# Four graph layers over 16 graphs on one core: degrees behind the wide drops, two row keys together, row numbers ahead of the next batch's scaling

## What is computed

```
layer 0: relu(D (A+I) D h W)          D = 1/sqrt(rowsum(A+I))
layer 1: [h, g h, g^2 h, g^3 h] W^T + b   g = d (A+I) d,  d = 1/(sqrt(rowsum)+1e-7)
layer 2: MLP(h + quantile aggregate of each node's neighbours)
         neighbours: A+I, from which rows with more than 10 neighbours lose every k-th one,
         in both directions; weighted sum of the 0.25, 0.5 and 0.75 quantiles, per feature
layer 3: A (h W) + b
```

## Time and profile before

| | us |
|---|---|
| median of 3 executions | 2806.65 |
| lowest, highest | 2795.49, 2807.34 |
| profiled execution, its own time | 2827.46 |
| its span, first to last instruction | 2825.7 |
| PE busy | 1535.0 (54%) |
| DVE busy | 1625.1 (58%) |
| ACT busy | 462.6 (16%) |
| POOL busy | 1299.3 (46%) |

### The profile page before, as it was taken

One profiled execution on the slowest core, in us unless ns is written; L12 is line 12 of the kernel. 1 busy time (PEld: TensorE's weight loads), 2 busy tenths in 40 slices (PEclk: granted clock), 3 DMA queues, 4 the chain that ended last, 5 costly groups with the idle time before them and its releaser, 6 DMA issues.

```text
span 2825.7 us, 24253 instructions
## 1 busy us (share of the span) xinstructions
PE 1535.0 (54%) x8885; PEld 858.3 (30%) x8997; DVE 1625.1 (58%) x2443; ACT 462.6 (16%) x756; POOL 1299.3 (46%) x1196
## 2 busy tenths in 40 slices
PE   3735637556374655638366464836636375565232
PEld 2412414323142332314233241423314243233111
DVE  2511827649285574928467383755828376494926
ACT  3101212102021120202112020210302121020000
POOL 1072370735527173552717447172643707265550
PEclk9766658667586766759577676866768586777555
DMA  3122130313213131321313123131322313112120
GB/s 99 54 25 53 46 55 21 75 11 86 19 40 62 24 75 12 83 22 34 67 20 77 15 53 54 29 69 8 88 18 50 55 22 75 10 23 20 23 24 4
DMA packets 106610, 120.13 MB, mean 43 GB/s; under 512 B 71486, under 2 KB 71614, under 8 KB 106430
## 3 DMA queue, kind: packets, MB, share of 16 engines
q0 software_dynamic: 36864, 37.82, 14.2%
q1 hardware_dynamic: 69566, 79.98, 9.2%
HBM read 109.27 MB, written 8.45 MB: 42 GB/s over the span
## 4 chain that ended last, share of the span: by engine, by line
DVE 40%; PE 24%; issue 18%; another core or an unknown queue 15%; ACT 2%; DVEq 1%; POOL 0%; DMA 0%; POOLq 0%; ACTq 0%; SPq 0%
PE ps_tr L596 7%; DVE lists L1181 4%; DVE slots L1001 4%; PE ps_tr L604 4%; DVE slots L1000 3%; PE ps_prod L615 3%; PE ps_tr L585 2%; PE ps_misc L775 2%; DVE slots L1008 2%; DVE slots L1009 2%; DVE xc L977 1%; DVE stat L979 1%; DVE stat L976 1%; PE ps_misc L704 1%
## 5 line engine op out<-in xcount | busy, mean ns | idle before, releaser
L403 POOL DMA_INDIRECT slots<-h_rows,row_no x1152 | 1287.4, 1118 | 1433.2 <-DVEq L1187 1087.0
L596 PE MATMUL ps_tr<-adj_t,y_mid 128*128 128x512 bf16 x960 | 301.7, 459 | 223.7 <-issue 121.3
L1223 DVE TENSOR_TENSOR y_mid<-ps_prod,scales 128x512 f32<-128x512 f32 x48 | 33.2, 692 | 554.2 <-remote 407.5
L448 ACT ACTIVATE columns_t<-ps_tr 128x512 f32<-128x512 f32 (+1 forms) x192 | 113.0, 595 | 1409.2 <-PE ps_tr L604 888.7
L596 PEld LDWEIGHTS ps_tr<-adj_t,y_mid 128*128 128x128 bf16 x1024 | 105.6, 112 | 471.1 <-issue 416.0
L1181 DVE MAX8 lists<-ps_key 128x8 f16<-128x1024 f32 x128 | 157.8, 1233 | 112.8 <-PE ps_key L685 69.4
L585 PE MATMUL ps_tr<-h_t,w_l_sb 65*128 65x512 f32 x192 | 151.3, 896 | 107.6 <-issue 76.1
L695 PE MATMUL ps_misc<-parts_w,select_t 128*128 128x64 bf16 x384 | 36.7, 220 | 268.1 <-issue 229.3
L472 ACT ACTIVATE adj_n<-adj_f 128x1024 f16<-128x1024 f32 x128 | 134.3, 1050 | 229.1 <-remote 80.7
L604 PE MATMUL ps_tr<-adj_t,low 128*64 128x512 bf16 x1024 | 157.9, 419 | 16.9 <-issue 16.6
L615 PE MATMUL ps_prod<-both_ident,columns_t 128*128 128x64 f32 x768 | 107.9, 297 | 101.6 <-issue 91.6
(11 more groups left out here) (210 smaller groups left out, 2539.2 us busy)
## 6 DMA issues: line engine op xcount, KB each, us to landing
adj_f<-in_adj SPq DMA_DIRECT2D x128, 512.0 KB
slots<-h_rows,row_no POOLq DMA_INDIRECT x1152
x<-in_x SPq DMA_DIRECT2D x16, 256.0 KB
h_rows<-h SPq DMA_DIRECT2D x16, 256.0 KB, 2.9
out<-x SPq DMA_DIRECT2D x16, 256.0 KB
xc<-in_L_gnn_W SPq DMA_DIRECT2D x1, 64.0 KB
w_sb<-in_L_gnn_W SPq DMA_DIRECT2D x2, 32.0 KB
h_rows<-zeros SPq DMA_DIRECT2D x2, 32.0 KB, 1.5
```

The costliest lines, as they stand in the source:

```text
L403: pool.indirect_dma_start(out=slots[:, slot_of(par, s), t * C:(t + 1) * C], out_offset=None, in_=table[par][:, :], in_offset=bass.Indirect ...
L448: act.activation(dst, view, ACT.Copy, scale=scale).then_inc(tr_free, 1)
L596: nc.tensor.matmul(dst[:, :], top_halves(pair_of)[:, j, :], adj_t[g % 3][:, columns[j]], start=(j == 0 and not begun), stop=False)
```

## The change

On PE, rows 0 and 1 are made one after the other, ahead of the turning back of v3, and row 3 ahead of mlp_rows. On DVE, degrees(n) moves from ahead of v1 to behind wide_drops(b); the row lists 3 to 7 each stand one place earlier among the norms; and row_numbers(b) stands ahead of norm_apply("norm0") and split of batch n.

```diff
 PE
                     pe.wait_ge(dropped_ready, b + 1)
                     row_keys(b, 0)
+                    row_keys(b, 1)
                     turned_back("v3", "v3", b, both_ident, False)
-                    row_keys(b, 1)
                     cross_drops(b)
                     row_keys(b, 2)
                     count_over(b)
+                    row_keys(b, 3)
                 if c is not None:
                     mlp_rows(c)
                 if b is not None:
-                    row_keys(b, 3)
                     row_keys(b, 4)
                     row_keys(b, 5)
 DVE
                     wide_sum(c)
-                if n is not None:
-                    degrees(n)
                 if b is not None:
                     propagate(b, "v1")
...
                     wide_drops(b)
+                if n is not None:
+                    degrees(n)
                 row_lists(0, 2)
                 if b is not None:
                     layer1_out(b)
...
                     flag_crowds(b)
+                row_lists(3, 4)
                 if c is not None:
                     add_mlp(c)
                     norm_stats(x[c % 4], z)
-                row_lists(3, 4)
+                row_lists(4, 5)
                 if c is not None:
                     norm_apply("norm3", c, z)
                     split(z_mid, low_z)
                 if b is not None:
                     norm_stats(x[b % 4], tiles(h2[b % 2]))
-                row_lists(4, 5)
+                row_lists(5, 6)
                 if b is not None:
                     norm_apply("norm2", b, tiles(h2[b % 2]))
                     dve.sem_inc(h2_ready, 1)
-                row_lists(5, 6)
+                row_lists(6, 7)
                 if n is not None:
                     dve.wait_ge(x_loaded, (n + 1) * 16)
                     norm_stats(x[n % 4], y)
-                row_lists(6, 7)
+                row_lists(7, 8)
+                if b is not None:
+                    row_numbers(b)
                 if n is not None:
                     norm_apply("norm0", n, y, d0[n % 2])
                     split(y_mid, low)
-                row_lists(7, 8)
-                if b is not None:
-                    row_numbers(b)
```

## The result

The changed kernel took **2696.66 us** (median of 6 executions, 2663.03 to 2762.86) against 2806.99 us for the kernel before, run beside it (6 executions, 2795.49 to 2825.8): ratio 0.9557, 95% interval 0.9485 to 0.9629. The medians are 110 us apart, six times the 18 us forecast. The profiled execution took 2674.01 us, span 2672.2.

The account below looks back on a forecast made before the run. Bound: a standstill tied to the gather. Summed: -2.73 + 0.3 + 0.4 + 0.1 = -1.9, +0.7 given back = -1.2 us a turn, 15 times: -18, giving 2788 us; own range 2776 to 2800, whole 2768 to 2824.

Parts of the forecast that it names:

- The bound: Loop from gather start to gather start: v2 held 118 to 121 us by the gather, then 48 to 49 us of work.
- The rival by which it follows PE: Hold before v1 and v2 follows PE, not the gather: 0 to +0.7 us a turn, 2809 us most likely; chance 0.22.
- (a): Row numbers ahead of the next batch's norm_apply and split on DVE: -2.73 us between v2 and the next gather start.
- (b): Row 3's keys ahead of mlp_rows on PE: DVE gets the MLP later, net +0.3 us a turn.
- (d): Norm 3 and its split behind row 4's list, delaying PE's h3.0 and row 6's keys: +0.4 us, between 0 and 1.0.
- (c): Rows 0 and 1 together on PE: row 1's list no longer waits for keys, 1.2 us gained, already used in (b).
- The slower rival: Row 3's keys cost about 2.0 us at the lower clock: +1.5 us a turn, 2829 us; chance 0.18.
- (e): Degrees moved between the wide drops and row 0's list on DVE: 0.94 us covered by idle time, no gain, 0.6 to spare.
- (f): DMA queues: the store of h2, released 1.4 us later, still lands ahead of the gather's start, covered by 4 us.
- (g): POOL's first gather issues beside three DVE operations of 0.69 us: +0.1 us, between 0 and 1.1.
- What is late next: PE reaches v1 about 2 us later against the gather's start, so v2 comes later: 0.7 us given back each turn.

Follow-up runs that it names:

- e11: Kernel before, with only 44 of a gather's 72 indirect DMAs issued (rows of odd tiles not brought): 2292.3 us against 2829.65.
- e8: Kernel before with degrees(n) alone moved behind wide_drops(b), on chip C: 2828.76 us, 0.9992 of the kernel before.
- e9: Kernel before with only row 7's list and row_numbers moved ahead of norm_apply norm0 and its split, on chip C: 2774.18 us, ratio 0.9804.
- e6: Changed kernel with the old order of row keys and lists 3 to 6, degrees and row numbers still moved, on chip B: 2682.27 us, ratio 0.9497.
- e7: Changed kernel with row 3 behind mlp_rows again and lists 3 to 6 at their old places, on chip B: 2664.9 us, ratio 0.9559.
- e5: The changed kernel again, on chip B: 2720.89 us, 0.9692 of the kernel before.
- e4: Changed kernel with degrees(n) back ahead of v1, on chip A: 2136.13 us, 1.0226 of the kernel before.
- e2: Kernel before with only row 7's list and row_numbers moved ahead of norm_apply norm0 and its split, on chip A: 2101.85 us, ratio 1.0037.
- e3: Kernel before with only the new order of row keys on PE and row lists 3 to 6 on DVE, on chip A: 2154.88 us, ratio 1.0316.
- e1: Kernel before with degrees(n) alone moved behind wide_drops(b), on chip A: 2100.19 us, 1.0038 of the kernel before.
- e10: The changed kernel again, on chip C: 2780.7 us, 0.9741 of the kernel before.
- e12: e7 with row 7's list and the row numbers also ahead of norm_stats of batch n, on chip D: 2673.29 us against 2801.61 of the kernel before.
- e14: e7 with spread_wide taking one bfloat16 part of three, on chip D: 2663.57 us, 0.943 of the kernel before.
- e16: Kernel before with adjacency loads cut to 8 of 1024 columns from batch 4 on: 2650.78 us, 0.9372 of the kernel before.

## Why the prediction was wrong

**The bound** was read rightly: a standstill tied to the gather, with its end at the gather's end (e11). The rival by which it follows PE falls. But the prediction read two turns, and took both v1 and v2 as caught in every one; v1 was caught to that end in most turns only (59.3 us behind gather 4 in the kernel before).

**(a) Row numbers, -2.73 in the last part.** Right: the tail fell by 2.5 us from e8 to e9 (36.0 to 33.5) on one chip.

**(b) to (d) Keys, +0.7 with the first list's gain in it.** Mis-sized. Rows 0 and 1 together brought 2.0 us of tail (e6 33.5 to e7 31.5) where I had 1.2. Row 3 ahead of the MLP, with the lists' new places, cost 3.9 us (e7 to e5, 31.5 to 35.5) where my sum has 1.9 (0.3 and the 1.2 already used up in (b), 0.4 in (d)). The net is +1.9 (e6 to the changed kernel) in place of +0.7. In the means of the long turns most of it lies ahead of the MLP: from row 0's list to it e6 has 11.07 us, the changed kernel 13.65, which without row 3's list (1.38) is +1.2 where (b) and (c) have +0.3. The rest is row 6's list, which waited 0.76 us in place of 0.15: +0.6 where (d) has +0.4, within its bounds. What (b) had too small is the time of row 3's keys. I took 1.14 us from row 0's keys, made at a granted clock of 1.00 (stretch 1619 to 1622), with two L681 matmuls in 0.59 us. In the changed kernel's short turn the clock was 0.50 (stretch 879 to 884) and row 3's two took 1.03; the MLP began behind them only (timeline of PE, changed kernel, row 3 and mlp_rows):

```profile
880.55 1.03 PE L681 MATMUL ps_key<-select_t,dropped 128*128 128x512 bf16 x2 [1.81 <-DVEq L1113]
...
882.48 0.60 PE L772 MATMUL ps_misc<-bias_rows,prefix 3*128 3x512 bf16 x1
```

Row 2's list ended at 879.20 + 1.23 = 880.43, so mlp_rows began 2.05 us behind it, where the forecast has 1.05 (1628.6 to 1629.65); DVE used the MLP 4.24 us after its start, as forecast, with the forecast wait of 2.9. The tail of the changed kernel, 35.4, is only 0.3 us below that of before. The slower rival's price for the keys (about 2.0 us, at the lower clock) was right, then. The keys' order costs 1.6 to 3.2% on chip A (e4 against e2, e3 against before); on the others it didn't decide.

**(e) Degrees.** Right as far as tested: alone they bring nothing (e8, 0.9992; on chip A they cost 0.4%, e1). The step for their cover held too: in the long turn behind gather 3 row 0's wait behind them was 0.42 us where 0.6 was forecast, and row 1's list followed row 0's with none.

**(f) Queues.** Right: all 16 waits of POOL for a gather's start still end with the row numbers (897.1, 16), none with the store of h2.

**(g) POOL's first issues.** The first two took 1.23 us and 1.15 us (762.74 above, and the next) against 0.94: 0.5 us together in place of 0.1. It is so in each of gathers 1 to 14; gather 15's, in the turn with no next batch and so without the three operations, took 0.95 and 0.94. The Trainium skill, page SBUF — State Buffer, section Who interferes with whom, would have it at 0; the trace disagrees again.

**What is late next: the step that failed.** I had v1 and v2 caught in every turn and priced a later v1 at +0.7. In the long turns v2 came 1.8 us earlier against the gather's start, not later (115.4 against 117.2), and in six turns v1 and v2 were not caught at all: -21.3 us each. The long ones gained 1.9, near the forecast's 1.2, but by luck: the tail gave 0.3 where my sum has 1.9, and row 0's list came 1.6 us earlier (129.6 against 131.2) where it has 0.7 later. Had all been long, the span would have shrunk by 153.5 - 6 x 19.4 = 37 us, more than my own range allows (31 below the median of before) and within the whole one (39). On chip C this is what happened: e10's profiled execution has no short turn (its shortest lasts 153.7 us), and its span is 36 us below e8's (2793.3 against 2829.6). That the second kind exists stood in the trace of before, which I read for two turns only. Timeline of its POOL (starts of gathers 14 and 15), and v1 and v2 between them:

```profile
2490.98 0.94 POOL L403 DMA_INDIRECT slots<-h_rows,row_no  x1 [64.45 <-DVEq L1187]
...
2632.81 0.94 POOL L403 DMA_INDIRECT slots<-h_rows,row_no  x1 [35.76 <-DVEq L1187]
```
```profile
2547.33 0.69 DVE L1223 TENSOR_TENSOR y_mid<-ps_prod,scales 128x512 f32<-128x512 f32 x1 [3.49 <-issue]
...
2559.75 0.69 DVE L1223 TENSOR_TENSOR y_mid<-ps_prod,scales 128x512 f32<-128x512 f32 x1 [0.59 <-issue]
```

141.8 us, with v1 at 56.3: a short turn, the only one, and the only one with no next batch to load. And behind gathers 4 and 9 of the same trace v1 had slipped through (at 59.3 and 63.2 us) and v2 was caught. A rival "some turns slip v1 and v2 through", at 25 us less for each, was to be had from it.

**What stays open.** Why moving the row numbers makes short turns is not shown. The eleven profiles with the move on holding chips (those of the table and e12, e14) have 30 short turns in 143, the two without it (before, e8) none in 26. But these two stem from two chips, and on one of them, C, the kernels with the move have only 1 in 26. They come unevenly, too: executions of one such kernel spread over 0.9% (e9) to 3.7% (the changed one). Since the move starts the gather earlier against the loads, it may do a little of what e16 does wholly; that was not tried by itself. What holds PE beside a gather, and why not on chip A, is open too. In the standstill of the earlier trace rows PE's matmuls stand 1.4 to 2.8 us apart, each wait ended by "issue", and DVE takes v1 36.8 us after PE's record of it ends: PE is slowed and its signals come late, and the profile names no cause. Slow loading of code is not seen: the packets of the profile's queues of kind "instruction" took at most 1.9 us in the kernel before (1.5 in e1 on chip A), and none lies in that standstill.

**The better version.** e7's order (degrees, numbers, rows 0 and 1 together, row 3 left behind mlp_rows) was faster than the kernel before on three chips that hold PE, and than the changed kernel on the one where both ran: beside the changed kernel on chip B 2664.9 against 2720.89, and 0.9467 and 0.9611 of the kernel before on D and E. e6's order, with all key products left as before, may be as good. On a chip like A it wasn't run; its parts e1 and e2 each cost 0.4% there.

## What to carry to other kernels

List every turn's distance before you reason from two: one odd turn can be the other state of the whole loop, and a small shift may flip many. Where a stall ends at a fixed distance from an event, two things have value, less work between its end and the next event, and more of the chain done before it begins; work moved round a loop brings nothing where no stall is in it. And ahead of a product that another engine waits for, put nothing that itself waits for that engine's last result: here it lengthened two waits.

## What the runs showed of the hardware

- One kernel took 2089.89 us on one chip and 2797.89 to 2829.65 on five others, with the gather's issues about equally long (some 105 us). In the standstills shown PE had 6.40 us of work in 36 and 4.43 in 22; on that one chip 30.16 in 36.
- The hold's end follows the number of indirect DMAs: with 72 it lay at 110.1 to 110.6 us behind the start in the short turns of the changed kernel, with 44 at 69.4 to 70.2 (e11).
- An indirect DMA's issue took 1.23 and 1.15 us beside DVE operations of 0.69 us, and 0.94 without them.
- With the adjacency's loads cut to 8 columns of 1024, the order of before took 0.9372 of its time (e16).
